# Second attention: the first-pass scores of two heads in the two halves of the TensorE array's rows

## The reference

```python
qkv = jnp.einsum('bsd,ed->bse', x, Wqkv)
q, k, v = jnp.split(qkv, 3, axis=-1)
...
logits = jnp.einsum('bihd,bjhd->bhij', q, k) * scale + pos_bias[None]
attn = jax.nn.softmax(logits, axis=-1)
out = jnp.einsum('bhij,bjhd->bihd', attn, v).reshape(B, S, D)
return jnp.einsum('bsd,ed->bse', out, Wout)
```

## Time and profile before

| | us |
|---|---|
| median of 3 runs | 2325.03 (2323.05 to 2331.76) |
| profiled execution, its time | 2327.71 |
| its span | 2325.9 |
| TensorE busy | 1985.4 |
| VectorE busy | 1502.4 |
| ScalarE busy | 1078.8 |
| GpSimd busy | 807.6 |

### The profile page before, as it was taken

How to read it: one execution, slowest core, us unless ns; L and a number is a source line. 1 busy time by engine, 2 the same in 40 slices (tenths; PEclk the granted TensorE clock), 3 DMA queues, 4 the chain that set the end, 5 groups by cost and what they waited for, 6 DMA issues and landing times. The chain is left out here.

```text
span 2325.9 us, 49229 instructions
## 1 busy us (share of the span) xinstructions
PE 1985.4 (85%) x15436; PEld 1034.3 (44%) x15436; DVE 1502.4 (65%) x4596; ACT 1078.8 (46%) x2723; POOL 807.6 (35%) x827
## 2 busy tenths in 40 slices
PE   8488787877388499999999999999999999679886
PEld 6255555655356133334333333334333433356554
DVE  6268878888511577777767767677677767233276
ACT  3355565565133045555555555455555555322221
POOL 4458888888400302221222122212221120100176
PEclk9689999999699699999999999999999999889998
DMA  3453232222187222322132213322232211144332
GB/s 111 153 181 109 105 104 100 75 104 98 45 229 221 91 72 80 100 84 95 61 97 92 87 61 96 95 85 86 72 103 82 96 59 64 56 140 158 115 104 86
DMA packets 127737, 235.72 MB, mean 101 GB/s; under 512 B 17622, under 2 KB 45286, under 8 KB 126966
## 3 DMA queue, kind: packets, MB, share of 16 engines
q1 hardware_dynamic: 118440, 208.51, 27.2%
q0 software_dynamic: 9072, 24.41, 3.7%
HBM read 185.88 MB, written 121.95 MB: 132 GB/s over the span
## 5 line engine op out<-in xcount | busy, mean ns | idle before, releaser
L1622 ACT ACTIVATE c_pT<-c_u 128x512 f32<-128x512 f32 x1024 | 574.6, 596 | 552.1 <-PE c_u L1429 552.1
L1777 DVE CUSTOM_DVE_ANT_0 c_sums<-c_s,bias 128x512 f32<-128x512 f32 x1024 | 665.1, 687 | 254.2 <-PE c_s L1411 229.5
L1411 PE MATMUL c_s<-c_kst,c_qst 126*128 126x512 bf16 x1024 | 319.0, 389 | 16.9 <-issue 11.5
L1429 PE MATMUL c_u<-spread_line,c_pick 128*32 128x512 bf16 x4096 | 317.2, 387 | 0.0
L1443 PE MATMUL c_o<-c_pT,c_vst 128*32 128x256 f32 x4096 | 310.9, 381 | 0.6 <-ACT c_pT L1622 0.5
L1421 PE MATMUL c_u<-c_qst,c_kst 128*128 128x512 bf16 x1024 | 307.7, 381 | 0.2 <-ACT c_pT L1622 0.2
L523 ACT ACTIVATE v<-a_bank,gain 128x64 f32<-128x64 f32 x768 | 166.4, 345 | 54.9 <-DVE vp L737 54.9
L1367 POOL DMA_INDIRECT zs_d<-c_xs,c_slot x64 | 63.4, 991 | 328.0 <-DMA zs_d<-in_zeros 190.6
L1443 PEld LDWEIGHTS c_o<-c_pT,c_vst 128*32 128x32 f32 x4096 | 123.1, 110 | 107.4 <-ACT c_pT L1622 4.0
L389 PE MATMUL a_bank<-wv,xT 128*128 128x512 f32 x256 | 154.1, 690 | 19.1 <-ACT v L523 14.2
L590 POOL TENSOR_TENSOR q<-q,vp 128x1024 f32<-128x1024 f32 x48 | 125.0, 2604 | 105.6 <-DVE vp L737 104.8
(11 more groups left out here) (266 smaller groups left out, 2901.3 us busy)
## 6 DMA issues: line engine op xcount, KB each, us to landing
xs_d<-in_zeros SPq DMA_DIRECT2D x16, 2048.0 KB
zs_d<-in_zeros SPq DMA_DIRECT2D x16, 2048.0 KB, 10.0
c_kst<-parts_d SPq DMA_DIRECT2D x192, 96.0 KB
c_qst<-parts_d SPq DMA_DIRECT2D x192, 96.0 KB
parts_d<-c_parts SPq DMA_DIRECT2D x32, 384.0 KB, 3.1
d_w<-in_wd SPq DMA_DIRECT2D x24, 384.0 KB, 3.2
b_w<-in_wb SPq DMA_DIRECT2D x24, 321.0 KB, 4.6
bias_d<-line_d SPq DMA_DIRECT2D x16, 448.0 KB
```

The costliest lines, as they stand in the source:

```text
L1411: nc.tensor.matmul(s_ps[bank_of(n)][:], qst[0:ROWS_MAX, h, t * P:(t + 1) * P], kst[0:ROWS_MAX, h, :], start=True, stop=True).then_inc(sem( ...
L1429: mm = nc.tensor.matmul(u_ps[bank_of(n)][ARRAY * k:ARRAY * (k + 1), :].rearrange("k (t q) -> k t q", t=T), pick[:], line[:, G * j + i, T - ...
L1622: nc.scalar.activation(pT[n // G % 2][:, n % G, :], u_ps[bank_of(n)][:], ACT.Exp).then_inc(sem("exp_done"), 1)
L1777: v.tensor_tensor_reduce(sums[n % 2][:], s_ps[bank_of(n)][:], bias, 1.0, -3.0e38, ALU.add, ALU.max, top_s[j % 2][:, k:k + 1]).then_inc(sem ...
```

## The change

The groups stay, but the four heads of a group are now laid out in two ways. The first two ("low") keep their nine blocks in rows 0 to 71 and their maxima in rows 126 and 127. The last two ("high") have the blocks (0, 0) to (2, 1) in rows 64 to 127, the block (2, 2) in rows 0 to 7, and their maxima in rows 62 and 63. The first pass now runs over 64 rows alone, rows 0 to 63 for a low head, rows 64 to 127 for a high one. The product of the smallest parts, (2, 2), is thereby left out of the maxima; since the same maximum is subtracted above and below the fraction of the softmax, this only moves the scale of both. The second pass is over all 128 rows as before. `unit` hands out the heads in the order 0, 2, 1, 3, so that the two units of a slot are a low and a high head; VectorE's maxima and ScalarE's targets follow this order.

A stack now takes 14 DMAs, seven for each of `kst` and `qst` (three for the low heads, four for the high ones), each for at most 24 rows of 1024 elements. The maxima come in with two DMAs, and the rows of -1 with two. The clearing of the stacks at the start covers 128 partitions and not 64.

```diff
+    HALF = P // 2
+    MAX_AT = (P - 2, HALF - 2)
+    BLOCK_ROWS = PARTS * HD
+    PAIRED = (0, 2, 1, 3)
+    STACK = 16 * 2 * (2 * PARTS + 1)
...
         def unit(n):
 
             j, n = n // TILES, n % TILES
-            return j, n // G, n % G
+            return j, n // G, PAIRED[n % G]
...
-                    for st, w, strides in ((kst, 1, (0, part)), (qst, 0, (part, 0))):
+                    for st, w, outer, inner in ((kst, 1, 0, part), (qst, 0, part, 0)):
+                        base = (2 * s.par + w) * PARTS * part
+                        low, high = G * j, G * j + G // 2
                         for a in range(PARTS):
-                            src = bass.AP(io["parts_d"].tensor,
-                                          (2 * s.par + w) * PARTS * part + a * strides[0] + j * G * N,
-                                          [[strides[1], PARTS], [H * N, HD], [1, G * N]])
-                            sp.dma_start(st[a * PARTS * HD:(a + 1) * PARTS * HD, G * j:G * j + G, :].rearrange("r h n -> r (h n)"), src
+                            src = bass.AP(io["parts_d"].tensor, base + a * outer + low * N,
+                                          [[inner, PARTS], [H * N, HD], [1, G // 2 * N]])
+                            sp.dma_start(st[a * BLOCK_ROWS:(a + 1) * BLOCK_ROWS, low:high, :].rearrange("r h n -> r (h n)"), src
+                                         ).then_inc(sem(f"stack_in{j}"), 16)
+                        for row, a, c, count in ((HALF, 0, 0, 3), (HALF + BLOCK_ROWS, 1, 0, 3), (HALF + 2 * BLOCK_ROWS, 2, 0, 2), (0, 2, 2, 1)):
+                            src = bass.AP(io["parts_d"].tensor, base + a * outer + c * inner + high * N,
+                                          [[inner, count], [H * N, HD], [1, G // 2 * N]])
+                            sp.dma_start(st[row:row + count * HD, high:high + G // 2, :].rearrange("r h n -> r (h n)"), src
                                          ).then_inc(sem(f"stack_in{j}"), 16)
...
-                    sp.dma_start(qst[ROWS_MAX:P, G * j:G * j + G, :].rearrange("r h n -> r (h n)"),
-                                 io["tops_d"].rearrange("a i p -> a (i p)")).then_inc(sem(f"m_in{j}"), 16)
+                    for k, row in enumerate(MAX_AT):
+                        h = G * j + G // 2 * k
+                        sp.dma_start(qst[row:row + 2, h:h + G // 2, :].rearrange("r h n -> r (h n)"),
+                                     io["tops_d"][:, TILES // 2 * k:TILES // 2 * (k + 1), :].rearrange("a i p -> a (i p)")).then_inc(sem(f"m_in{j}"), 16)
...
-                    nc.tensor.matmul(s_ps[bank_of(n)][:], qst[0:ROWS_MAX, h, t * P:(t + 1) * P], kst[0:ROWS_MAX, h, :],
+                    row = HALF * (2 * i // G)
+                    nc.tensor.matmul(s_ps[bank_of(n)][:], qst[row:row + HALF, h, t * P:(t + 1) * P], kst[row:row + HALF, h, :],
                                      start=True, stop=True).then_inc(sem("s_ps"), 1)
...
-                    nc.scalar.activation(pT[n // G % 2][:, n % G, :], u_ps[bank_of(n)][:], ACT.Exp).then_inc(sem("exp_done"), 1)
+                    nc.scalar.activation(pT[n // G % 2][:, PAIRED[n % G], :], u_ps[bank_of(n)][:], ACT.Exp).then_inc(sem("exp_done"), 1)
...
-                v.memset(kst[64:P], 0.0).then_inc(sem("pad_ready"), 1)
-                v.memset(qst[64:P], 0.0).then_inc(sem("pad_ready"), 1)
+                v.memset(kst[:], 0.0).then_inc(sem("pad_ready"), 1)
+                v.memset(qst[:], 0.0).then_inc(sem("pad_ready"), 1)
```

More of the change, by code:

```diff
@@ L1122, in attention_two @@
     ROWS_QK = PARTS * PARTS * HD
-    ROWS_MAX = P - 2
-    STACK = 16 * 2 * PARTS
+    HALF = P // 2
[3 more added lines that the diff above has]
+    STACK = 16 * 2 * (2 * PARTS + 1)
     VC = HD + 1
@@ L1325, in _ @@
                 sp.wait_ge(sem("pad_ready"), 2)
-                sp.dma_start(kst[ROWS_MAX:P].rearrange("r h n -> r (h n)"), io["minus_d"]).then_inc(sem("minus_in"), 16)
+                for k, row in enumerate(MAX_AT):
+                    sp.dma_start(kst[row:row + 2].rearrange("r (j i) n -> r j (i n)", i=G)[:, :, G // 2 * N * k:G // 2 * N * (k + 1)],
+                                 io["minus_d"][:, H // 2 * N * k:H // 2 * N * (k + 1)].rearrange("r (j n) -> r j n", j=GROUPS)).then_inc(sem("minus_in"), 16)
                 load(at(1))
@@ L1417, in below @@
                     if n % TILES == 0:
-                        pe.wait_ge(sem(f"m_in{j}"), 16 * s.b + 16)
+                        pe.wait_ge(sem(f"m_in{j}"), 32 * s.b + 32)
                     need(pe, sem("exp_done"), freed(s, n))
@@ L1595, in _ @@
                 pe.wait_ge(sem("pad_ready"), 2)
-                pe.wait_ge(sem("minus_in"), 16)
+                pe.wait_ge(sem("minus_in"), 32)
                 for n in range(2 * LEAD):
```

## The result

The changed kernel took 2317.26 us (2315.13 to 2322.02), the kernel before 2325.84 us beside it: ratio 0.9965, interval 0.995 to 0.998. That is 8.6 us less where 29.8 were forecast, and inside the half per cent that was named as no change, though the interval leaves out 1: the gain is real and small. The profiled execution took 2318.80 us, 8.9 less than that of before.

What follows compares the result with a forecast made beforehand. TensorE was taken to set the pace; -109.1 + 67.3 + 5 + 2 + 5 = -29.8 us on the median of 2325.03 gave a forecast of 2295 us, range 2245 to 2328.

Steps and rivals of the forecast that it cites:

- item 1: In 496 first-pass pairs in slots, the second matmul starts with the first, 0.22 us less each: -109.1 us.
- item 2: 748 new changes between half and full rows around the first pass, at 0.09 us each: +67.3 us.
- w: Price of one change of form of TensorE's array, taken for rows as 0.09 us from column-form changes.
- item 3: Late in each batch, slots without spare for VectorE give back 0.3 us: +5 us over 15 batches.
- item 4: Value products wait for ScalarE about once a batch, losing one slot's gain there: +2 us.
- item 5: More DMA issues in SyncE's queue make the first tops late ahead of slot 0: +5 us, bounds 0 and 6.
- B: Rival: a row-form change is dearer than a column one, 0.11 to 0.13 us, giving 2308 to 2325 us; chance 0.08.
- C: Rival, slower: a pair's second matmul starts late, 2345 us partial, 2397 without overlap; chances 0.08 and 0.07.
- A: Rival: a row-form change is cheap, 0 to 0.05 us, giving 2240 to 2270 us; chance 0.22.

## Why the prediction was wrong

The mechanism was right and the direction too, but the gain was less than a third of the forecast, since two terms of the sum were mis-sized the same way: the price of a change of form, by 12 us, and what VectorE gives back, by 8.

1. **The pair** (item 1, -109.1 us): right. The two halves start together, 0.39 us for the pair. By the Trainium skill, TensorE: Matmul & The Clock Gate, Measured speedup vs the span model, they start some 4 ns apart; the trace, whose pair is no longer than one matmul to the hundredth, agrees.
2. **The price of a change of form** (item 2, w = 0.09): this step failed by its size. The plain slot gained 0.11, not 0.13, and the slot after other work 0.01, not 0.04. The step from the pair to the second pass costs 0.10 us more than without a change (0.32 for 0.22), and the step from the second pass to the bias products grew by 0.01 besides (0.54 at 1421.22 to 1421.76, for 0.52); in the run with both heads in the same half a plain slot pays 0.10 in all. 244 x 0.11 + 252 x 0.01 = 29.4 us are left of 41.8, so item 2 is 79.7 us and not 67.3: 0.107 for each of the 748, where 0.09 was taken from the changes of column form. By the Trainium skill, TensorEngine Tiling (Array Packing), Key Properties, changing the tiling mode drains TensorE. The trace agrees for rows as for columns that a change costs time, 0.10 us here; whether a drain is what takes it the trace does not show.
3. **What VectorE gives back** (item 3, +5): this step failed too, by less in us and by more as a factor. It is 0.39 (slot 15) + 0.18 (slot 26) + 0.27 more than before (slot 27) = 0.84 us a batch, some 13 us. I looked for the place where TensorE already waited, and judged the rest by busy shares. Two things escaped me: the second matmul of a pair now wants its bank 0.22 us earlier relative to the first, on top of the shorter slot; and the round of banks breaks at slot 15, where the bank is wanted after two units.
4. **ScalarE** (item 4, +2): no wait on TensorE's stream came of it; nothing.
5. **SyncE** (item 5, +5): right, 4.0 us. The four stacks held the queue for 30.8 us, 7.7 each as worked out, since an issue did not get cheaper with half the bytes. They ended at 820.9 and not at 824, because in this execution the first began 3.1 us earlier than before, at 790.1.

The sum by these is -109.1 + 79.7 + 13 + 4 = -12.4 us; in the stage the traces show 1203.6 against 1193.3 us from the first first-pass matmul to the last second-pass one, 10.3 less. Of the other 2 us 1.7 are the first three slots of batch 0, which together took 1.4 us more where 0.2 less were due, at the lower clock. That this clock is SyncE's doing is not shown, since the run with the first tops early has it too. Outside the stage the changed kernel's execution is 1.4 us longer (1.5 less ahead of it, 3.0 more behind), which no part of the change explains; so 8.9 us are left in all.

Of the rivals, B (a dearer change of row form) came nearest: it led from w = 0.11 on to 2308 to 2325, and the measured time lies there. The whole price of 0.107 a change is just under its band, and about 12 of the 21 us that were missing are due to it; VectorE's 8 us took the time the rest of the way, so that B met the time is in part luck. C, the pair not together, is refuted, and A, a cheap change, by the run with the same half.

## What to carry to other kernels

Matmuls in two halves of the rows run together at no cost, but count the changes of form that they bring: here each cost half of what a pair gained. So group the work by form. Moving the full-row work from ahead of the half-row pair to behind it took 38 us off the slots, where the change itself had taken 14; but 27.5 us came off the kernel before by the same move, so look for such an order before the change as well. With the order right and VectorE relieved in both, the two halves are worth 30.7 us. And when two matmuls start at once, they want both output banks at once: look at the order in which banks come round before judging the slack by busy shares.

## What was not expected

- A change of form costs FP32 matmuls more: four transposes directly behind one take 0.49 us to the next matmul, 0.44 elsewhere, and one of them loads weights for 0.14 us, a BF16 matmul for 0.10. That the longer load is the reason was not tested.
- An issue of a DMA on SyncE costs 0.36 us for the keys' stack and 0.65 to 0.68 for the queries' whether it moves 96 or 48 KB. What sets the two apart in the program is a source that reads each row three times.
- On one chip VectorE and ScalarE stood still together for 3 to 4 us at recurring moments, in both traces taken there. The kernel before took 2369 us there, 1.8% more than beside the changed kernel at first; it has no trace there, so whether it stood still is not known.
